# Layer 0's GELU written as Erf and one VectorE multiplication, so that ScalarE keeps one table set

## The chip, the cores and the metric

The kernel runs on one core of a Trainium2 chip. The metric is the device time of one execution in microseconds. The engines are PE (TensorE), DVE (VectorE), ACT (ScalarE), POOL (GpSimd) and SP (SyncE, which issues DMAs).

## What is computed

The input x is 8 x 128 x 128 (batch, time, channel). Four blocks follow each other, each of the form x = x + ffn(cond(x)). Cut to what matters here, layer 0 is:

```python
# cond of layer 0 (t_emb is the condition, one row per batch element)
shared = silu(xf @ w1) * (xf @ w3) @ w2
s = sigmoid(concatenate([xf, tf]) @ router_W)
# the top 2 of s + router_bias; gates are their s, divided by the sum (1/2 each where the sum is below 1e-9)
h = gelu(einsum('nc,ech->enh', xf, W1e), approximate=False)      # 8 experts, 128 wide
routed = einsum('ne,enc->nc', combine, einsum('enh,ehc->enc', h, W2e))
c = (shared + routed) / 3
# ffn of layer 0
probs = sigmoid(c @ router_w.T)
# the top 2 of probs, divided by their sum
h = square(relu(einsum('td,edw->tew', c, W1e)))
x = x + einsum('ted,te->td', einsum('tew,ewd->ted', h, W2e), combine)
```

Layer 1 is a GRU over time and a feed-forward part with 8 experts and exact GELU, layer 2 a gated linear part with 8 experts and exact GELU, and layer 3 a tanh recurrence followed by a 12-expert mixture with exact GELU.

## The kernel before

The 1024 columns (time x batch) are cut into four chunks of 256 (32 steps of time). The work up to layer 2 is a list of units, and each takes one slot n. C units are the cond part of layer 0 (C0 and C1 the silu pair, C2 to C5 two experts each), F units its feed-forward part, A and B units layers 1 and 2. Every engine goes through the slots in the same order. The first 44 slots (A_START = 44) hold layer 0: C0 to C5 of the first chunk are slots 0 to 5, then C0 to C3 of the second chunk (6 to 9), F0 to F5 of the first (10 to 15), C4 and C5 (16, 17); the third chunk's C0 to C3 are 18 to 21, F0 to F5 of the second 22 to 27, C4 and C5 28 and 29; the last chunk's C0 to C5 are 30 to 35, F of the third chunk 36 to 41, and two F units of the last 42 and 43.

In slot n PE does the up product of unit n (`project`, into PSUM bank U[n % 2], two halves in quarters 0 and 1) and the down product of unit n - 2 (`down`, into Y, in quarters 2 and 3). `project(n)` first waits until unit n - 2 has been taken out of its bank (`wait_hidden`, L1684). ACT applies the curve of unit n (`hidden`, L775) in quarter 2: for C0 a tanh into `act`, for C2 to C5 `Gelu` straight into `gated` (L783), for F units relu and, in quarter 3, the square (L797). DVE finishes C0 and C1 in `finish(n - 1)` (L1150) at quarter 0 of slot n. With the expert weights as scalars it adds the down products of slot n - 3 to accumulators `acc_a` and `acc_b` (L955, four operations of 128x128 in C2 to C5 and F0 and F1, two in F2 to F5). The down of a unit waits until the adds of the unit two before it have freed its Y bank.

At slot 2, quarter 0, DVE also does the router of the cond part: `scores_c`, and `route_c` for the first two tiles (L1471 to L1475); the other six tiles follow at slots 6 to 9. `take_sums` (L1189) writes the layer's output c0, which the F units read, four slots after C5, and the logits' copy one slot later. ACT then applies the sigmoid (`sigmoid_l0`, L799) at SIG_SLOT, that is slots 10, 22, 36 and 40, and DVE ranks them in eight quarters from the next slot's quarter 1 on (`route_f_quarter`, L1242).

From slot 20 to slot 43 the first 32 steps of the GRU run between the quarters (`beat`, L98): in four steps of every three slots, PE multiplies for the gates, ACT applies two tanh (L761, L763), DVE makes `rh`, PE multiplies, ACT applies a tanh (L767), and DVE's scan gives the new state (L1041). POOL makes the part of the state that is kept. The later steps go one per slot, with A and B units.

ACT's functions come from table sets, and a load is placed ahead of the first function that the loaded set does not hold. The kernel steers this by hand for some: `table_of` (L804) applies a function to one column so that its set is loaded there. It does so for Gelu at slots 27 and 42 (GELU_AGAIN) and for Sigmoid in quarter 2 of slot 22 (SIG_LATE), where the relu of slot 22 and its square are held back to slot 23, quarter 0, behind the sigmoid. The sigmoid of the third chunk waits until slot 36, quarter 0.

Of the kernel before, what the change touches and what calls it, by code (L numbers as in the profile page):

```python
# [1 line left out]

# [5 lines left out]
ALU = mybir.AluOpType  # L8
ACT = mybir.ActivationFunctionType
# [5 lines left out]
CHUNKS = T // CT  # L15
N = CT * B
# [4 lines left out]
F = 512  # L21
# [23 lines left out]
def layer_units(stream, k, first=0, last=LU):  # L45

    return [(stream, i, k) for i in range(first, last)]


UNITS = L0_UNITS[:-HOLD] + layer_units("A", 0) + L0_UNITS[-HOLD:]  # L50
# [5 lines left out]
AT = {u: n for n, u in enumerate(UNITS)}  # L56
A_START = AT["A", 0, 0]
C3 = AT["A", 0, CHUNKS - 1]
SIG_SLOT = [AT["C", 5, k] + 5 for k in range(CHUNKS)]
SIG_SLOT[2] = AT["C", 5, CHUNKS - 1] + 1  # L60
SIG_LATE = SIG_SLOT[1]
GELU_AGAIN = AT["F", 5, 1], A_START - 2
UP_HI_SLOTS = [8, 9] + [14 + e for e in range(E - 2)], [A_START + 4 + 2 * e for e in range(E)]
W1_SLOTS = [AT[stream, i, k] for k in (1, 2) for stream, i in zip("AAABBB", (7, 10, 13, 6, 7, 10))]

# [7 lines left out]
def unit(n):  # L73

    return UNITS[n] if 0 <= n < len(UNITS) else ("", 0, 0)
# [79 lines left out]
def m_of(*name):  # L155
    return M_PRO + X.index(name)
# [16 lines left out]

def made_by_act(n):

    return sum(stream in "FAB" or stream == "C" and i > 1 for stream, i, c in UNITS[:n + 1])


class OwnOrder:
# [11 lines left out]
def adaln_ffn_program(nc, a, out):  # L191
    with ExitStack() as ctx:
        def sb(name, shape, dtype=F32, scope=ctx):
            return scope.enter_context(nc.sbuf_tensor(name, shape, dtype))
# [4 lines left out]
        def psum(name):  # L199
            return ctx.enter_context(nc.psum_tensor(name, [P, 512], F32))  # L200

        def sem(name):
            return ctx.enter_context(nc.semaphore(name))
# [45 lines left out]
        c0 = (l2_in, z1m_c0[:, N:])  # L249
        l1_x, l2_x = parts("l1_x", [P, N]), parts("l2_x", [P, N])  # L250
        gated = sb("gated", [P, 4, 512])
# [47 lines left out]
        with ExitStack() as early:  # L299
# [4 lines left out]
            silu = sb("silu", [P, 512], scope=early)  # L304
            act = sb("act", [P, 512], scope=early)
# [91 lines left out]
        U = [psum("U0"), psum("U1")]  # L397
# [15 lines left out]
        m_full, m_free = sem("m_full"), sem("m_free")  # L413
        e_full, ga_full, gd_full = sem("e_full"), sem("ga_full"), sem("gd_full")
        l3_hid = sem("l3_hid")
        set_up = sem("set_up")
        l0_sig, silu_done = sem("l0_sig"), sem("silu_done")
# [308 lines left out]
        def _(sc):  # L726
# [3 lines left out]
            def load_small(loads):  # L730
                for dst, src in loads:
                    sc.dma_start(dst, src).then_inc(ld_small, 16)
# [42 lines left out]
            def hidden(n):  # L775
                stream, i, k = unit(n)
                if (stream, i) == ("C", 1) or not stream:
                    return
                sc.wait_ge(u_full, n + 1)
                if (stream, i) == ("C", 0):  # L780
                    nc.scalar.activation(act[:, :], U[n % 2][:, :], ACT.Tanh, scale=0.5).then_inc(e_full, 1)
                elif stream == "C":
                    nc.scalar.activation(gated[:, n % 4, :], U[n % 2][:, :], ACT.Gelu).then_inc(ga_full, 1)  # L783
                elif stream == "F":
                    nc.scalar.activation(relu[:, i % 2, :], U[n % 2][:, :], ACT.Relu).then_inc(relu_done, 1)
                else:
                    for h in range(2):
                        col = (stream == "B") * E * Q + 2 * i + h
                        last = nc.scalar.activation(gated[:, n % 4, h * N:(h + 1) * N], U[n % 2][:, h * N:(h + 1) * N],  # L789
                                                    ACT.Gelu, bias=b1T[:, col:col + 1])  # L790
                    last.then_inc(ga_full, 1)

            def square_l0(n):
                stream, i, k = unit(n)
                if stream == "F":
                    sc.wait_ge(relu_done, k * 6 + i + 1)
                    nc.scalar.activation(gated[:, n % 4, :], relu[:, i % 2, :], ACT.Square).then_inc(ga_full, 1)  # L797

            def sigmoid_l0(n):  # L799
                if n in SIG_SLOT:  # L800
                    sc.wait_ge(m_free, m_of("logits", SIG_SLOT.index(n)) + 1)
                    nc.scalar.activation(sig_a[:, 0:TILES * E], score[:, 0:TILES * E], ACT.Sigmoid).then_inc(l0_sig, 1)  # L802

            def table_of(func):  # L804

                nc.scalar.activation(table[:, :], ident[:, 0:1], func)  # L806
# [47 lines left out]
            for n in range(A_START):  # L854
                for quarter in range(4):
                    gates, cand_step = beat(n, quarter)
                    if gates is not None:
                        gru_gates_of(gates)
                    if cand_step is not None:
                        gru_cand_of(cand_step)  # L860
                    if quarter == 0 and n - 1 == SIG_LATE:
                        sigmoid_l0(n - 1)
                        hidden(n - 1)
                        square_l0(n - 1)
                    if quarter == 0 and n == SIG_SLOT[2]:
                        sigmoid_l0(n)
                    if quarter == 0 and n in GELU_AGAIN:
                        table_of(ACT.Gelu)
                    if quarter == 2 and n == SIG_LATE:
                        table_of(ACT.Sigmoid)  # L870
                    if quarter == 0:
                        mid_copies(n)
                    if quarter == 2 and n != SIG_LATE:
                        hidden(n)
                    if quarter == 3 and n == 0:
                        load_small(small_loads[9:])
                    if quarter == 3 and n == 1:
                        sigmoid_c()
                    if quarter == 3 and n not in (SIG_LATE, SIG_SLOT[2]):
                        sigmoid_l0(n)  # L880
                    if quarter == 3 and n != SIG_LATE:
                        square_l0(n)
                    if quarter == 3:
                        up_high(n)
            for n in range(A_START, SLOTS):
# [56 lines left out]
        def _(dve):  # L942
# [6 lines left out]
            def ts(out, in0, s1, op0, s2=None, op1=None):  # L949
                if op1 is None:  # L950
                    return v.tensor_scalar(out, in0, s1, None, op0)
                return v.tensor_scalar(out, in0, s1, s2, op0, op1)

            def stt(out, in0, scalar, in1, op0, op1):
                return v.scalar_tensor_tensor(out=out, in0=in0, scalar=scalar, in1=in1, op0=op0, op1=op1)  # L955
# [194 lines left out]
            def finish(n):  # L1150

                stream, i, k = unit(n)
                if (stream, i) == ("C", 0):
                    dve.wait_ge(e_full, k + 1)
                    stt(silu[:, :], act[:, :], 1.0, U[n % 2][:, :], ALU.add, ALU.mult).then_inc(silu_done, 1)
                if (stream, i) == ("C", 1):
                    dve.wait_ge(u_full, n + 1)
                    dve.wait_ge(silu_done, k + 1)
                    stt(gated[:, n % 4, :], silu[:, :], 0.5, U[n % 2][:, :], ALU.mult, ALU.mult).then_inc(gd_full, 1)

            def add_l0(n, part):

# [17 lines left out]
            def taken(*name):  # L1180
                dve.wait_ge(m_full, m_of(*name) + 1)
                return bank_of(*name)
# [6 lines left out]
            def take_sums(n):  # L1189

                if n == MID_SLOT + 1:
                    later_set_up()
                stream, i, k = unit(n - 4)
                if (stream, i, k) == ("C", 5, 0):
                    dve.wait_ge(m_free, m_of("mid", 2) + 1)
                if (stream, i, k) == ("C", 5, 1):
                    dve.wait_ge(m_free, m_of("mid", 3) + 1)
                if (stream, i) == ("C", 5):
                    ts(c0[k % 2][:, :], taken("c", k)[:, 0:N], 1.0 / 3.0, ALU.mult).then_inc(m_free, 1)
                if (stream, i) == ("F", 5):  # L1200
                    tt(x1[:, at(k * N, N)], xT[:, at(k * N, N)], taken("f", k)[:, 0:N], ALU.add).then_inc(m_free, 1)
                stream, i, k = unit(n - 5)
                if (stream, i) == ("C", 5):
                    v.tensor_copy(score[:, 0:S], taken("logits", k)[:, 0:S]).then_inc(m_free, 1)
# [367 lines left out]
        def _(pe):  # L1572
# [111 lines left out]
            def wait_hidden(n):  # L1684
                stream, i, k = unit(n)
                if (stream, i) == ("C", 0):
                    pe.wait_ge(silu_done, k + 1)
                elif (stream, i) == ("C", 1):
                    pe.wait_ge(gd_full, k + 1)
                else:  # L1690
                    pe.wait_ge(ga_full, made_by_act(n))

# [294 lines left out]
```

## Time and profile before

| | us |
|---|---|
| median of 3 runs | 599.39 |
| lowest, highest | 598.94, 599.4 |
| the profiled execution, its time | 599.04 |
| its span, first to last instruction | 597.3 |

The profile has a page (busy time and share of each engine, the chain of work that ended last) and views of the trace: the busy time by stretches, the timeline, the instructions by line, the waits. Times in the trace are counted from the start of the span. The time of a run exceeds the span by 1.7 us here. The busy shares are means over the whole span, and this change acts only on the first 44 slots, which end near 124 us.

### The profile page before, as it was taken

To read this page: it belongs to the slowest core of one execution; us is meant where nothing else is said; L and a number is where in the kernel's file an instruction comes from. 1 tells how busy PE (TensorE), PEld (TensorE's weight loads), DVE (VectorE), ACT (ScalarE), POOL (GpSimd) and SP (SyncE) were. 2 spreads that over 40 slices of the span, in tenths; PEclk is the share of its full clock that TensorE was granted. 3 is DMA by queue.
4 is the path that set the end of the run, shared out by engine and by line. 5 is a ranking of instruction groups with operands and counts; after the bars stand their busy time and mean duration, and the time that the engine had idled before them with its cause. 6 is when DMAs were issued, how large, how long until landed. Compare 5 with 4: busy or idle time off the path is not lost.

```text
span 597.3 us, 11431 instructions
## 1 busy us (share of the span) xinstructions
PE 584.0 (98%) x3978; PEld 538.1 (90%) x3978; DVE 356.5 (60%) x1199; ACT 287.1 (48%) x955; POOL 116.9 (20%) x340
## 2 busy tenths in 40 slices
PE   8899999999999999999999999999999999999996
PEld 8789889899999999999999999989999899898995
DVE  4965666865564455555654564479696763675414
ACT  3375645645665456555565556656833323302110
POOL 3334122111111111111211110000201311312410
PEclk9999999999999999999999999999999999999999
DMA  8999900002002010001010022380502003003000
GB/s 242 318 316 138 76 4 2 2 2 73 1 1 72 2 64 10 2 19 54 17 57 2 0 73 72 71 142 3 176 1 107 6 6 107 6 6 108 8 1 9
DMA packets 55297, 35.44 MB, mean 59 GB/s; under 512 B 29976, under 2 KB 48968, under 8 KB 54728
## 3 DMA queue, kind: packets, MB, share of 16 engines
q1 hardware_dynamic: 53216, 34.23, 24.2%
q10 hardware_dynamic: 2024, 0.48, 0.4%
q8 instruction: 31, 0.51, 0.4%
q14 instruction: 26, 0.21, 0.1%
HBM read 34.06 MB, written 0.64 MB: 58 GB/s over the span
## 4 chain that ended last, share of the span: by engine, by line
PE 86%; DVE 6%; issue 4%; ACT 2%; POOL 1%; DVEq 0%; POOLq 0%
PE Y L1574 35%; PE U L1574 32%; PE HH L1574 7%; PE ZR L1574 7%; PE M L1574 3%; DVE acc_a L955 2%; POOL scaled_lo L704 1%; DVE cmp_a L947 1%; DVE rh L955 0%; ACT L806 0%; ACT L802 0%; PE M L1590 0%; ACT gated L797 0%; DVE gated L955 0%; PE Y L1604 0%
## 5 line engine op out<-in xcount | busy, mean ns | idle before, releaser
L789 ACT ACTIVATE gated<-U,b1T 128x256 f32<-128x256 f32 x256 | 106.5, 472 | 0.3 <-PE U L1574 0.2
L1574 PE MATMUL U<-l_x_hi,l_up_hi 128*128 128x256 f32 x256 | 83.5, 326 | 0.0
L674 POOL TENSOR_SCALAR zh<-zr_s 128x8 f32<-128x8 f32 x128 | 26.4, 206 | 238.9 <-ACT zr_s L763 238.9
L771 ACT ACTIVATE h<-ZR,rnn_b 128x8 f32<-128x8 f32 x128 | 34.3, 268 | 78.9 <-PE ZR L1574 77.3
L1574 PE MATMUL U<-l_x_lo,l_up_hi 128*128 128x256 f32 x256 | 72.0, 281 | 0.0
L1574 PE MATMUL U<-l_x_hi,l_up_lo 128*128 128x256 f32 x256 | 71.7, 280 | 0.0
L1041 DVE TENSOR_TENSOR_SCAN h_gru<-blend,cand_keep 128x16 f32<-128x16 f32 x128 | 25.0, 195 | 77.7 <-ACT cand_keep L767 75.7
L1574 PE MATMUL Y<-gated,l_dn 128*128 128x256 f32 x256 | 69.8, 396 | 0.2 <-DVE product L947 0.2
L767 ACT ACTIVATE cand_keep<-HH 128x8 f32<-128x8 f32 x128 | 22.8, 178 | 92.4 <-PE HH L1574 92.4
L1574 PE MATMUL U<-scaled_hi,l_up_hi 128*128 128x256 f32 x192 | 57.6, 300 | 0.0
L1574 PE MATMUL U<-scaled_lo,l_up_hi 128*128 128x256 f32 x192 | 54.3, 283 | 0.0
L1574 PE MATMUL U<-scaled_hi,l_up_lo 128*128 128x256 f32 x192 | 54.2, 282 | 0.0
L1574 PEld LDWEIGHTS HH<-h_gru,gru_u 128*128 128x128 f32 x256 | 46.5, 190 | 7.7 <-DVE h_gru L1041 2.2
L1574 PEld LDWEIGHTS ZR<-h,rnn_w 128*128 128x128 f32 x256 | 43.3, 189 | 6.7 <-ACT h L771 2.3
L1574 PEld LDWEIGHTS U<-l_x_hi,l_up_lo 128*128 128x128 f32 x256 | 48.8, 191 | 0.1
L1574 PEld LDWEIGHTS U<-l_x_hi,l_up_hi 128*128 128x128 f32 x256 | 48.7, 190 | 0.1
L955 DVE SCALAR_TENSOR_TENSOR acc_a<-Y,mix,acc_a 128x128 f32<-128x128 f32 x96 | 33.7, 351 | 24.4 <-PE Y L1574 21.9
L1574 PEld LDWEIGHTS U<-l_x_lo,l_up_hi 128*128 128x128 f32 x256 | 48.2, 188 | 0.0
L1574 PEld LDWEIGHTS HH<-rh,gru_u 128*128 128x128 f32 x256 | 39.1, 188 | 9.7 <-DVE rh L955 7.9
L1574 PEld LDWEIGHTS Y<-gated,l_dn 128*128 128x128 f32 x256 | 44.1, 191 | 4.1 <-issue 0.6
L1574 PE MATMUL ZR<-h_gru,gru_u 128*128 128x8 f32 x256 | 47.1, 256 | 0.0
L1574 PE MATMUL HH<-rh,gru_u 128*128 128x8 f32 x256 | 39.8, 228 | 2.4 <-DVE rh L955 2.0
(277 smaller groups left out, 1352.4 us busy)
## 6 DMA issues: line engine op xcount, KB each, us to landing
l_bc<-dw SPq DMA_DIRECT2D x4, 1536.0 KB, 6.4
stage<-L_ffn_W_dram SPq DMA_DIRECT2D x4, 768.0 KB, 15.1
w_raw<-L_ffn_W_dram SPq DMA_DIRECT2D x12, 256.0 KB, 5.6
l_bc<-dmix SPq DMA_DIRECT2D x9, 256.0 KB, 3.8
l_bc<-dmix SPq DMA_DIRECT2D x3, 768.0 KB, 5.4
l_up_raw<-L_ffn_W_dram SPq DMA_DIRECT2D x1, 2048.0 KB, 11.5
l_up_raw<-L_ffn_w_dram SPq DMA_DIRECT2D x1, 2048.0 KB, 12.9
l_weighted<-dmix SPq DMA_DIRECT2D x3, 512.0 KB, 4.7
```

What stands on the lines that cost most here:

```text
L674: own(nc.gpsimd.tensor_scalar(zh[:, :], zr_s[:, 0, :], -0.5, 0.5, ALU.mult, ALU.add))
L704: nc.gpsimd.tensor_tensor(out=scaled[1][:, 2 * j:2 * j + 2, :].rearrange("p e n -> p (e n)"), in0=source[:, j % 2, :], in1=scaled[0][:, 2 ...
L767: nc.scalar.activation(cand, HH[:, at(N + step % CT * B, B)], ACT.Tanh).then_inc(gru_cand, 1)
L771: nc.scalar.activation(h3[:, at((step + 1) * B, B)], ZR[:, at(step % CT * B, B)], ACT.Tanh, bias=rnn_b[:, 0:1]).then_inc(rnn_h, 1)
L789: last = nc.scalar.activation(gated[:, n % 4, h * N:(h + 1) * N], U[n % 2][:, h * N:(h + 1) * N], ACT.Gelu, bias=b1T[:, col:col + 1])
L947: return v.tensor_tensor(out=out, in0=in0, in1=in1, op=op)
L955: return v.scalar_tensor_tensor(out=out, in0=in0, scalar=scalar, in1=in1, op0=op0, op1=op1)
L1041: v.tensor_tensor_scan(out=h_gru[:, at(step % CT * 2 * B, 2 * B)], data0=blend[:, :], data1=cand_keep[:, :], initial=0.0, op0=ALU.mult, op ...
L1574: return nc.tensor.matmul(out, lhsT, rhs, start=start, stop=stop, skip_group_check=shared)
```

## The change

C2 to C5 no longer use Gelu. ACT writes Erf(u / sqrt(2)) into the one buffer `act`, and DVE multiplies (act + 1) by U into `gated`, which is twice the GELU. The factor is made good in c0 (1/6 in place of 1/3), and C1's product is doubled too (1.0 in place of 0.5). The hand-made table steps go: the sigmoids of the second and third chunk stand in quarter 3 of slots 22 and 34 (SIG_SLOT as computed), the relu and square of slot 22 in their own quarters, and one Gelu is applied to a column at the end of slot 43. ACT waits, before each curve of a C unit, for DVE to have read the last one out of `act`. PE waits for C units on `gd_full` (DVE) in place of `ga_full` (ACT).

```diff
-SIG_SLOT[2] = AT["C", 5, CHUNKS - 1] + 1
-SIG_LATE = SIG_SLOT[1]
-GELU_AGAIN = AT["F", 5, 1], A_START - 2
...
 def made_by_act(n):
-    return sum(stream in "FAB" or stream == "C" and i > 1 for stream, i, c in UNITS[:n + 1])
+    return sum(stream in "FAB" for stream, i, c in UNITS[:n + 1])
+
+def made_by_dve(n):
+    return sum(stream == "C" and i > 0 for stream, i, c in UNITS[:n + 1])
+
+def curves_of_c(n):
+    return sum(stream == "C" and i != 1 for stream, i, c in UNITS[:n + 1])
...
                 sc.wait_ge(u_full, n + 1)
+                if stream == "C":
+                    before = max((m for m in range(n) if unit(m)[0] == "C" and unit(m)[1] != 1), default=None)
+                    if before is not None and unit(before)[1] == 0:
+                        sc.wait_ge(silu_done, unit(before)[2] + 1)
+                    elif before is not None:
+                        sc.wait_ge(gd_full, made_by_dve(before))
...
                 elif stream == "C":
-                    nc.scalar.activation(gated[:, n % 4, :], U[n % 2][:, :], ACT.Gelu).then_inc(ga_full, 1)
+                    nc.scalar.activation(act[:, :], U[n % 2][:, :], ACT.Erf, scale=math.sqrt(0.5)).then_inc(e_full, 1)
...
-                    if quarter == 0 and n - 1 == SIG_LATE:
-                        sigmoid_l0(n - 1)
-                        hidden(n - 1)
-                        square_l0(n - 1)
-                    if quarter == 0 and n == SIG_SLOT[2]:
-                        sigmoid_l0(n)
-                    if quarter == 0 and n in GELU_AGAIN:
-                        table_of(ACT.Gelu)
-                    if quarter == 2 and n == SIG_LATE:
-                        table_of(ACT.Sigmoid)
...
+                    if quarter == 3 and n == A_START - 1:
+                        table_of(ACT.Gelu)
...
-                    dve.wait_ge(e_full, k + 1)
+                    dve.wait_ge(e_full, curves_of_c(n))
...
-                    stt(gated[:, n % 4, :], silu[:, :], 0.5, U[n % 2][:, :], ALU.mult, ALU.mult).then_inc(gd_full, 1)
+                    stt(gated[:, n % 4, :], silu[:, :], 1.0, U[n % 2][:, :], ALU.mult, ALU.mult).then_inc(gd_full, 1)
+                if stream == "C" and i > 1:
+                    dve.wait_ge(e_full, curves_of_c(n))
+                    stt(gated[:, n % 4, :], act[:, :], 1.0, U[n % 2][:, :], ALU.add, ALU.mult).then_inc(gd_full, 1)
...
-                    ts(c0[k % 2][:, :], taken("c", k)[:, 0:N], 1.0 / 3.0, ALU.mult).then_inc(m_free, 1)
+                    ts(c0[k % 2][:, :], taken("c", k)[:, 0:N], 1.0 / 6.0, ALU.mult).then_inc(m_free, 1)
...
-                elif (stream, i) == ("C", 1):
-                    pe.wait_ge(gd_full, k + 1)
+                elif stream == "C":
+                    pe.wait_ge(gd_full, made_by_dve(n))
```

## Rows read from the trace of the kernel before

**Rows 1.** The page: busy time by engine, and the chain that ended last by engine.
```profile
PE 584.0 (98%) x3978; PEld 538.1 (90%) x3978; DVE 356.5 (60%) x1199; ACT 287.1 (48%) x955; POOL 116.9 (20%) x340
...
PE 86%; DVE 6%; issue 4%; ACT 2%; POOL 1%; DVEq 0%; POOLq 0%
```

**Rows 2.** Busy by stretch: length, each engine's busy us (instructions), clock, DMA share, GB/s.
```profile
12.10:21.00 8.90, 7.46 (x46) 6.42 (x46) 7.89 (x26) 5.07 (x8) 3.37 (x5) 1.00 1.13 325
...
38.00:51.70 13.70, 13.67 (x95) 12.88 (x95) 7.12 (x23) 9.16 (x16) 7.62 (x6) 1.00 1.32 211
```

**Rows 3.** The chain in order of time, 8 to 62 us: start, us, what.
```profile
21.01 1.13 PE Y L1574 x8
22.14 0.86 PE U L1574 x4
23.01 0.89 PE Y L1574 x8
...
29.33 1.12 PE U L1574 x4
...
31.08 1.28 ACT L802
...
32.62 0.85 DVE cmp_a L947
...
38.03 1.13 PE Y L1574 x8
...
51.75 0.18 ACT zr_s L761
```

**Rows 4.** The timeline, 12 to 52 us: start, us, engine, line, operation [idle before <- releaser].
```profile
15.17 1.13 PE L1574 MATMUL U<-h,l_up 128*128 128x256 f32 x4 [0.25 <-ACT gated L783]
...
19.40 0.17 DVE L947 TENSOR_TENSOR comb_x<-comb_x,mask 128x16 f32<-128x16 f32 x1
...
19.61 2.54 DVE L955 SCALAR_TENSOR_TENSOR acc_a<-Y,comb_x,acc_a 128x128 f32<-128x128 f32 x8
```

**Rows 5.** By line or tile: ns min/median/max, first and last start in us.
```profile
L783 ACT ACT_TABLE_LOAD  x2: 1283/1283/1283, 13.2 to 43.6; - x2
...
L802 ACT ACT_TABLE_LOAD  x2: 1283/1283/1283, 31.1 to 99.0; - x2
...
L806 ACT ACT_TABLE_LOAD  x3: 1283/1283/1283, 59.1 to 117.0; - x3
...
L781 ACT ACTIVATE act<-U x4: 592/597/597, 8.5 to 83.2; 128x512 f32<-128x512 f32 x4
L955 DVE SCALAR_TENSOR_TENSOR silu<-act,U x4: 661/684/689, 11.1 to 84.3; 128x512 f32<-128x512 f32 x4
```

**Rows 6.** Busy by stretch: slots 20, 23, 27, 33, 35, 38, 42.
```profile
51.79:54.59 2.80, 2.71 (x19) 2.17 (x18) 2.34 (x10) 1.44 (x6) 0.52 (x3) 1.00 1.69 142
...
60.55:64.11 3.56, 3.18 (x23) 2.62 (x22) 2.40 (x11) 2.97 (x11) 0.80 (x4) 1.00 1.51 121
...
73.10:76.13 3.03, 2.77 (x21) 2.48 (x20) 1.31 (x7) 2.81 (x9) 0.65 (x4) 1.00 0.05 12
...
89.92:92.60 2.68, 2.68 (x22) 2.57 (x22) 1.41 (x6) 1.20 (x5) 1.29 (x6) 1.00 0.00 0
...
95.89:98.65 2.76, 2.76 (x23) 2.56 (x22) 2.25 (x11) 1.41 (x6) 0.59 (x3) 1.00 0.00 0
...
104.51:107.97 3.46, 3.15 (x23) 2.54 (x22) 3.13 (x16) 1.98 (x8) 0.70 (x4) 1.00 0.00 0
116.62:119.64 3.02, 2.76 (x20) 2.46 (x20) 2.12 (x11) 2.80 (x9) 0.68 (x4) 1.00 0.00 0
```

**Rows 7.** The timeline of ACT at slot 44.
```profile
124.04 0.18 ACT L761 ACTIVATE zr_s<-HH 128x8 f32<-128x8 f32 x1 [1.43 <-PE HH L1574]
```

**Rows 8.** PE's waits, 0 to 52 us: total us, times, longest us.
```profile
PE Y L1574 <- DVE acc_a L955: 2.3, 3, 1.2
```

**Rows 9.** The timeline of PE at the start.
```profile
1.58 3.78 PE L1574 MATMUL HH<-ident 128*128 128x128 f32 x16 [1.58 <-POOL ident L603]
```

More of the change, by code:

```diff
@@ L1 @@
 from contextlib import ExitStack
+import math
 import concourse.bass as bass
@@ L860, in _ @@
                         gru_cand_of(cand_step)
-                    if quarter == 0 and n - 1 == SIG_LATE:
-                        sigmoid_l0(n - 1)
-                        hidden(n - 1)
-                        square_l0(n - 1)
-                    if quarter == 0 and n == SIG_SLOT[2]:
-                        sigmoid_l0(n)
-                    if quarter == 0 and n in GELU_AGAIN:
-                        table_of(ACT.Gelu)
-                    if quarter == 2 and n == SIG_LATE:
-                        table_of(ACT.Sigmoid)
                     if quarter == 0:
                         mid_copies(n)
-                    if quarter == 2 and n != SIG_LATE:
+                    if quarter == 2:
                         hidden(n)
@@ L878, in _ @@
                         sigmoid_c()
-                    if quarter == 3 and n not in (SIG_LATE, SIG_SLOT[2]):
+                    if quarter == 3:
                         sigmoid_l0(n)
-                    if quarter == 3 and n != SIG_LATE:
+                    if quarter == 3:
                         square_l0(n)
+                    if quarter == 3 and n == A_START - 1:
+                        table_of(ACT.Gelu)
                     if quarter == 3:
```

## The prediction

> **What bounds the kernel now.** I read the page first: PE is busy 98% of the span, DVE 60%, ACT 48%, and the chain that ended last is 86% PE, 6% DVE and 2% ACT [rows 1]. So ACT's table loads can give back only what lies on that 2%, or what they delay on the small share of the others. The change acts only before slot 44, that is before about 124 us. I therefore read that stage in parts. From 12.1 to 21.0 us DVE is busy 7.89 of 8.90 us and PE 7.46, so the opening of layer 0 is DVE's. From 38.0 to 51.7 us PE is busy 13.67 of 13.70 us and DVE 7.12: there DVE has room [rows 2].
>
> The chain in order of time says the same. From the first router's scores to 21.01 us it runs through DVE (routing of the first chunk, then the expert adds), and PE resumes at 21.01. It is PE's to 29.33; then relu, a table load of 1.28 us at 31.08 (the chain counts all of it), and DVE again from 32.62 until PE takes over at 38.03 [rows 3]. The third view is the engines' timeline: PE starts U of slot 4 at 15.17, having waited 0.25 us (so from 14.92, when the down product of slot 1 ends) for ScalarE's GELU of slot 2. DVE's last routing operation of the first two tiles starts at 19.40 and ends at 19.57 [rows 4]. Between these two rows lies the main step.
>
> **What goes.** In layer 0 ACT loads a table eight times after the first Tanh: once for the first sigmoid (L739), and seven more: two at L783, two at L802, three at L806, 1283 ns each [rows 5]. After the change Sigmoid, Tanh, Erf, Relu, Square and Copy share one set, so the load at L739 stays and one Gelu load at the end of slot 43 takes the place of these seven: six fewer, 7.7 us of ACT. What each is worth at the end:
> - The load at 13.2 delays U of slot 4 by 0.25 us at most, and what follows waits longer for DVE: 0.
> - The load at 31.08 is on the chain. Without it the sigmoid waits for the logits' copy, which DVE will deliver late (below). I count it there.
> - The load at 43.6 lies where PE is the bound [rows 2]: 0.
> - In the GRU stage a slot takes 2.68 us when nothing disturbs it (slot 33). Slots 27, 36 and 42, each of which has a load between two GRU gates, take 3.02 to 3.04 (the first and the last of the three stand in [rows 6]): 0.35 us each, 1.05 in all, not 1.28 each, since the GRU's own round trip hides the rest.
> - The load at 59.1 ends before the next gates are due. But slot 23 takes 3.56 us, with the sigmoid, the held-back relu and its square packed ahead of the GRU candidate. Spread as the change has them, I take back 0.5 (between 0 and 0.88, its excess over slot 33).
> - The new load at slot 43 fills ACT's idle time there: the next gates start at 124.04 after 1.43 us of idle ACT [rows 7]; 1.28 and the one-column Gelu (0.2) fill it: 0.1 us lost.
>
> Of the load itself the rows show 1283 ns, and the chain has nothing else at it: 31.08 and 1.28 us, then the sigmoid and at 32.62 the compare [rows 3]. The Trainium skill ("ScalarE: Activation LUTs", What ACT_TABLE_LOAD costs) agrees on 1283 ns but adds about 1380 ns of drain for each switch. By that figure the three loads inside the GRU would give an estimated 4.1 us more, and the forecast would be no change. Between the load's end (32.36) and the compare lie 0.26 us, which hold the sigmoid and no such drain, so the sum goes by 1283 ns; the other case is among the rivals.
>
> **What comes.** Sixteen expert units (four in each chunk) get a DVE product of 128x512 from act and U, and the same shape took 684 ns [rows 5]. ScalarE's Erf takes a GELU's place; the trace has no Erf, and I take 0.60 from the Tanh of this shape (597 ns, [rows 5]) as for the GELU: between nothing and twice this, a bound that matters for two of them. More important is where DVE finds them. finish(n - 1) stands at quarter 0 of slot n, and at slot 2 DVE does the whole routing of the first two tiles inside that quarter. So the product of slot 2 can't start before 19.57 us, though its Erf is ready near 14. PE's U of slot 4 waits for gated of slot 2 (it reuses that bank), and everything is queued behind it. The steps, with PE's 0.87 us for a project and 0.89 for a down ([rows 3], at 22.14 and 23.01):
> - Slot 2's product 19.6 to 20.3. PE starts U of slot 4 at 20.4 in place of 15.17.
> - `act` is one buffer, so the Erf of slot 3 waits for that product: 20.3 to 20.9; product 21.0 to 21.65. Erf of slot 4 21.7 to 22.3; product 22.3 to 23.0. DVE idles 0.67 us before each of these two.
> - Then slot 2's four adds (eight took 2.54 us, [rows 4]) to 24.3, slot 5's product to 25.0, slot 3's adds and a mask to 26.5. PE's down of slot 5, which waits for these adds, starts at 26.5 in place of 23.01: +3.5.
> - DVE goes on without a pause and has some 0.3 us more delay than PE by then; slot 8's product (0.7) goes in ahead of c0: PE's U of slot 10 starts at 33.9 in place of 29.33, +4.6. Slot 9's product goes ahead of the logits' copy: +5.3 there. Now the load at 31.08 is missing, so the sigmoid is at +4.0 and the first compare, 32.62 before, near 36.8: +4.2. GpSimd's subtractions will stand elsewhere beside that compare (0.85 us here), which may give up to 0.4 back.
> - From there to 38.03 DVE is dense with unchanged work, then PE is the bound until the GRU starts: the products of slots 16 and 17 fit beside it. I take +4.0 at 51.7 us, with 2.5 and 5.5 as ends (the first if PE and DVE overlap better by two products, the second if no part of the shift is recovered).
>
> In the GRU stage eight products remain. In slots 21, 22, 29, 30, 33 and 34 they meet few adds. Before, slot 20 has such a product already (C1 of the third chunk) and takes 2.80 us, against 2.76 for slot 35 without one [rows 6]. This is 0.04, but DVE's products stand at other places of the GRU beat in four of the six, where DVE must have the reset ready some 0.8 us after the update. Ends 0 and 0.68; I take 0.2 each, nearer to the row: 1.1. Slots 35 and 36 get a product, four adds and, since the third sigmoid moves from slot 36 to 34, its ranking; slot 38 loses it. Ranking with four adds cost 3.46 against 2.76 in slots 38 and 35, so 0.7 moves and the product adds some 0.2 each: +0.4. Sum of the stage: 1.1 + 0.4 + 0.1 - 1.05 - 0.5 = 0.05. The new waits of ACT on silu_done and gd_full bind only in slots 3 to 5: elsewhere the product runs a quarter or two before ACT's next curve. SP's queue isn't touched and its loads are not awaited by PE here. POOL's GRU work follows ACT's gates.
>
> **The sum.** +4.0 + 0.05 = +4.05 on the profiled execution's 599.04 (span 597.3): 603.1, and 0.35 us more on the median of 599.39: 603.4. Behind slot 44 PE is the bound (98% overall), so the shift reaches the end whole.
>
> **Rivals.**
> - The slow clock, chance 0.25. PE would be idle from 14.9 to 20.4 us, 5.5 us, which nothing in the trace before resembles: its waits for DVE up to 52 us are three of 2.3 us together, the longest 1.2 [rows 8]. At the start, out of idleness, 16 products took 3.78 us, 236 ns each, against 111 ns for the same shape at 23.01 [rows 3, 9]: the lower level of 1.2 GHz by their durations, though the granted clock reads 1.00. If PE drops to it, U of slot 4 and the next two products take about 0.9 us more each, and slot 3's adds end some 2 us later: 605.4. The Trainium skill ("TensorE: Matmul & The Clock Gate", Part 1) says that an idle PE returns to half rate and needs sustained work to leave it.
> - The loads win, chance 0.10: if each of the four loads that stand in the GRU stage gave its full 1.28 (5.1 with slot 23), the one at 31.08 too, and the first slots lost only two products (1.4) because PE's queue isn't held up: 599.4 - 6.4 + 1.4 + 1.1 = 595.5. It decides where the product of slot 2 runs before the routing; the order of the code speaks against it.
> - The loss is caught, chance 0.05: PE's three waits before 38 us, 2.3 us together [rows 8], absorb most of it and the GRU gains 1.5, or a switch holds ACT longer than its row shows, so that the three slots give their 1.28 each and more: 599.6 to 600.5 either way.
> - The change doesn't do what it says, 0.05: if Erf and Sigmoid lie in different sets, the sigmoids keep their loads: +1.3 to +2, 605.
> - Otherwise, 0.55, the forecast.
>
> **The numbers.** A measurement of this kernel can tell 0.2%, 1.2 us, from no change. The low end takes the smaller opening loss (2.5 in place of 4.0) and products in the GRU slots that cost nothing but in 35 and 36 (1.1 less), plus half of what slot 23 and the three loads may still give beyond my price: 600.3. The high end is the clock case with 1.1 of the 1.5 by which the opening may be dearer: 606.5. The winning case and the tails are left out, nearly 2 in 10. Faster 0.10, same 0.05, slower 0.85.
>
> **What would show it.** Right: a DVE product at 19.6 directly behind comb_x; PE idle some 5 us before U of slot 4; PE's U of slot 10 near 34 and the first GRU gates near 55.7 (51.75 before, [rows 3]); three table loads in all; slots 27, 36 and 42 near 2.7. Slow clock: products of the 128x128 shape near 230 ns after 20.4. Wrong: U of slot 4 before 17 us, or a gain of over 2 us between the first gates and slot 44, or more than three loads.

## The result, and the profile after

The changed kernel takes 604.56 us (median of 6) against 599.69 for the kernel before in the same runs; the ratio is 1.0094, with a 95% interval from 1.0083 to 1.0105. By the ratio it is 5.0 to 6.3 us slower. The two medians alone give 4.9 us (1.0081), a little under that interval, so the size is known to some 0.7 us. The profiled execution took 604.4 us, its span is 602.7.

The page, the two lines that answer to [rows 1], and the clock row of its second part:

```profile
PE 586.1 (97%) x3978; PEld 540.2 (90%) x3978; DVE 365.1 (61%) x1215; ACT 280.8 (47%) x947; POOL 117.8 (20%) x340
...
PEclk9799999999999999999999999999999999999999
...
PE 89%; DVE 8%; issue 2%; ACT 1%; POOL 0%; DVEq 0%; POOLq 0%
```

ACT lost 6.3 us of work and DVE gained 8.6, and the chain moved the same way: ACT 2% to 1%, DVE 6% to 8%. New is the 7 in the row of the clock. The timeline of the opening shows where it comes from (start, us, engine, line, operation, idle before and what ended it); it answers to [rows 4]:

```profile
13.51 0.60 ACT L798 ACTIVATE act<-U 128x512 f32<-128x512 f32 x1
...
19.69 0.17 DVE L954 TENSOR_TENSOR comb_x<-comb_x,mask 128x16 f32<-128x16 f32 x1
...
19.89 0.69 DVE L962 SCALAR_TENSOR_TENSOR gated<-act,U 128x512 f32<-128x512 f32 x1
20.64 2.07 PE L1584 MATMUL U<-h,l_up 128*128 128x256 f32 x4 [5.41 <-DVE gated L962]
20.68 0.60 ACT L798 ACTIVATE act<-U 128x512 f32<-128x512 f32 x1 [6.57 <-DVE gated L962]
21.31 0.69 DVE L962 SCALAR_TENSOR_TENSOR gated<-act,U 128x512 f32<-128x512 f32 x1 [0.72 <-ACT act L798]
22.50 1.91 PE L1584 MATMUL Y<-l_dn,gated 128*128 128x128 f32 x8
```

Slot 2's Erf is ready at 14.11, its product stands behind the last routing operation and starts at 19.89, and PE sat idle for 5.41 us before U of slot 4. These four matmuls then take 2.07 us (1.13 in [rows 4]), and the eight of the down 1.91, where the timeline of the kernel before has 1.05:

```profile
16.13 1.05 PE L1574 MATMUL Y<-l_dn,gated 128*128 128x128 f32 x8
```

The stretches of the same opening (length, busy us and instructions of PE, PEld, DVE, ACT and POOL, granted clock, DMA share, GB/s) give the reason:

```profile
12.40:15.20 2.80, 2.80 (x18) 2.43 (x17) 2.28 (x8) 1.34 (x3) 0.00 (x0) 1.00 1.19 286
15.20:20.60 5.40, 0.03 (x1) 0.00 (x0) 4.96 (x14) 0.00 (x0) 3.35 (x5) 0.74 1.11 334
20.60:22.50 1.90, 1.86 (x4) 1.51 (x5) 0.69 (x1) 0.60 (x1) 0.00 (x0) 0.50 1.05 376
22.50:24.50 2.00, 2.00 (x10) 2.00 (x9) 0.73 (x2) 0.60 (x1) 0.00 (x0) 0.50 1.20 288
24.50:26.00 1.50, 1.50 (x11) 1.34 (x11) 1.18 (x4) 0.53 (x1) 0.00 (x0) 0.96 1.05 270
```

While PE idles its granted clock falls, and from 20.6 to 24.5 us it is 0.50, the lower level of 1.2 GHz, although PE is busy again. Only then does it return.

PE's first matmul of each slot gives the shift against the kernel before, slot by slot. The first of slot 20 starts at 57.37 (51.79 before, +5.58), that of slot 24 is at +4.97, of slot 28 at +4.29, of slot 31 at +4.73, of slot 35 at +4.74, of slot 38 at +6.51, of slot 39 at +5.84 and that of slot 44, at 130.10, is at +5.54. So the opening costs 5.58 and the GRU stage nothing (-0.04), and behind slot 44 the rest of the span takes back only 0.1. Three stretches of it, slots 23, 27 and 42, answer to three of [rows 6], and slots 35 and 36 stand behind them:

```profile
66.12:69.08 2.96, 2.92 (x23) 2.57 (x22) 2.41 (x11) 1.94 (x7) 0.78 (x4) 1.00 1.13 98
77.89:80.42 2.53, 2.53 (x21) 2.43 (x20) 1.38 (x7) 1.55 (x7) 0.65 (x4) 1.00 0.00 1
122.45:125.19 2.74, 2.74 (x20) 2.47 (x20) 2.12 (x11) 1.54 (x7) 0.71 (x4) 1.00 0.00 0
100.63:104.41 3.78, 3.11 (x23) 2.64 (x22) 3.34 (x14) 1.45 (x6) 0.80 (x4) 1.00 0.01 2
104.41:107.91 3.50, 2.81 (x21) 2.40 (x20) 3.22 (x14) 1.37 (x6) 0.40 (x2) 1.00 0.00 0
```

Slot 23 takes 2.96 us in place of 3.56, slot 27 2.53 in place of 3.03, slot 42 2.74 in place of 3.02: there the loads and the packed sigmoid are gone. In slot 35 DVE is busy 3.34 of 3.78 us and in slot 36 3.22 of 3.50: each has a product, four adds and a part of the ranking.

### The profile page after: what moved, and what is told of

Its sections match the earlier page's. It is cut to its first block, busy times and chain, and to the rows that moved or that the text cites. A ratio compares the mean times of both kernels' runs of the same rounds, so it can differ in the third digit from the quotient of the medians.

```text
span 602.7 us, 11458 instructions
## 1 busy us (share of the span) xinstructions
PE 586.1 (97%) x3978; PEld 540.2 (90%) x3978; DVE 365.1 (61%) x1215; ACT 280.8 (47%) x947; POOL 117.8 (20%) x340
## 4 chain that ended last, share of the span: by engine, by line
PE 89%; DVE 8%; issue 2%; ACT 1%; POOL 0%; DVEq 0%; POOLq 0%
PE Y L1584 36%; PE U L1584 33%; PE ZR L1584 8%; PE HH L1584 7%; PE M L1584 3%; DVE acc_a L962 2%; DVE gated L962 1%; DVE cmp_a L954 0%; DVE rh L962 0%; PE Y L1614 0%; DVE comb_x L954 0%; DVE l_x_lo L954 0%; PE M L1600 0%; DVE h_gru L1048 0%; DVE cmp_b L954 0%
```

## The experiments

In the readings below, "shift" is the start of a slot's first matmul against the kernel before. The first layer's start itself varies by some 0.4 us between executions (U of slots 2 and 3 starts at 12.13 in the kernel before, 12.44 in the changed one, between 11.96 and 12.47 in the others); where shifts of the opening are compared, this is taken out and the number is called net. The changed kernel's net shift at slot 20 is 5.58 - 0.31 = 5.27.

A net shift is good to some 0.3 to 0.5 us, since DVE's routing starts by its own path. Its first operation on the sigmoid's output starts at 13.24 in the kernel before. It is 0.31 later in the changed kernel and 0.36 in pe_warm, which agrees with U of slot 2. But it is 0.61 later in products_early (U of slot 2: 0.31) and 0.45 later in sig36 (U of slot 2: 0.09 earlier). Each profile is also one execution, and not always a typical one.

**pe_warm: products that nothing reads, in PE's wait.** Each of the 24 calls makes two matmul instructions of the trace, x48.

```diff
+                    if (n, quarter) == (4, 0):
+                        keep_busy(24)
                     if quarter < 2:
                         project(n, (quarter,))
```

> The changed kernel, with 24 idle products (128x128 into HH, which nothing reads before the GRU) in PE's queue ahead of U of slot 4, to fill its wait from 15.2 to 20.6 us. Theory A (the drop of the granted clock to 0.50 after the wait is a cost of its own): U of slot 4 still starts near 20.6, its four matmuls take some 1.0 us in place of 2.07, the down of slot 5 starts near 26.9 in place of 28.8, and the time is 1.3 to 2.0 us under the change, about 603.0. Theory B (DVE bounds these slots anyway, the clock costs nothing): 604.4 to 604.8.

602.81 us, ratio 1.0056 (1.0041 to 1.0071). The timeline and the stretch after the wait:

```profile
15.15 5.52 PE L1584 MATMUL HH<-ident 128*128 128x128 f32 x48
20.69 1.13 PE L1584 MATMUL U<-h,l_up 128*128 128x256 f32 x4
...
20.60:22.50 1.90, 1.89 (x13) 1.71 (x13) 0.72 (x2) 0.96 (x2) 0.00 (x0) 1.00 1.05 378
```

U of slot 4 starts at the same time (20.69) and takes 1.13 us in place of 2.07, the clock stays at 1.00, and slot 20 is at +4.04, net 3.74. The wait is the same, only its effect on the clock is gone: theory A, and the clock's own share of the opening is 5.27 - 3.74 = 1.53 us in these two executions.

**product2_early and products_early: the products of slots 2 and 3 inside the routing.**

```diff
-                        finish(n - 1)
+                        if n not in (3, 4):
+                            finish(n - 1)
                         if n == 2:
                             scores_c()
                             route_c(range(TILES), (0,))
+                            finish(2)
                             add_l0(1, 0)
+                            finish(3)
                             route_c(range(TILES), (3, 4, 5))
```

This is products_early; product2_early has finish(2) alone there and leaves finish(3) at its place.

> The changed kernel, with the product of slot 2 moved on DVE's queue from behind the routing of the first two tiles (slot 3) to its middle, right behind the ranking (slot 2). Nothing else moves. Theory A (the place of this product in DVE's order opens the wait): U of slot 4 starts near 16.7, no clock drop, but the product of slot 3 still stands behind the routing, so U of slot 5 waits to about 21.3; 2.0 to 3.0 us under the change, about 602. Theory B (the loss is DVE's work alone, sixteen products of 0.69): no change, 604.6, since DVE does the same work.

601.57 us, ratio 1.0039 (1.0025 to 1.0052). Theory B (no change) is refuted. U of slot 4 starts at 16.65 and U of slot 5 at 20.68, after waits of 1.40 and 2.01 us, as expected. But the clock did fall, a little later:

```profile
18.00:20.00 2.00, 0.68 (x7) 0.48 (x5) 1.73 (x9) 0.00 (x0) 1.60 (x4) 1.00 1.02 375
20.00:22.00 2.00, 1.32 (x5) 1.14 (x6) 1.27 (x3) 0.60 (x1) 0.00 (x0) 0.85 1.04 385
22.00:24.00 2.00, 2.00 (x10) 1.92 (x9) 1.93 (x7) 0.60 (x1) 0.00 (x0) 0.50 1.19 290
```

So "no clock drop" was wrong: two shorter waits with some work between them bring it as well.

> The changed kernel, with the products of slots 2 and 3 both put into the middle of slot 2's routing on DVE (behind the ranking, and behind the copy of slot 1's down). PE then has no wait over 2.5 us and its clock stays. What is left of the opening's loss is the six products of slots 2 to 5, 8 and 9 on a DVE that is the bound. Theory A (this work is most of the +4.0 that stay without the clock drop): the first GRU slot still starts 2.7 to 3.3 us later than before (51.79), 601.0 to 601.8. Theory B (the order on DVE's queue was most of it): it starts less than 1.5 us later, under 600.5.

600.07 us, ratio 1.0010 (1.0001 to 1.0019): almost all of the loss is gone, and theory A is refuted in size. Slot 20 is at +2.05, net 1.74, where 2.7 to 3.3 was expected. Theory B's time (under 600.5) holds; its bound of 1.5 for slot 20 is missed by the start of U of slot 2 and met by the start of the routing (2.05 - 0.61 = 1.44). PE's granted clock is 1.00 from 12.4 to 32.0 us. With the same operations as the changed kernel and no clock drop, the order on DVE's queue is worth 3.74 - 1.74 = 2.00 us, or 2.2 by the start of the routing. Six products of 0.69 (4.1 us of DVE) cost 1.4 to 1.7 when they stand where they are ready, since part of them falls into idle time of DVE; that this is the reason is argued, not measured. The medians put more on the order: pe_warm lies 3.6 us over the kernel before and this run 0.7, and its profiled execution (600.62) was one of its slowest. So the order is the largest part by either measure, and its size is 2 to 3 us.

**gelu0: the first chunk as before.** ACT's GELU for slots 2 to 5, Erf and products from slot 8 on.

```diff
+                elif stream == "C" and k < 1:
+                    nc.scalar.activation(gated[:, n % 4, :], U[n % 2][:, :], ACT.Gelu).then_inc(ga_full, 1)
                 elif stream == "C":
                     nc.scalar.activation(act[:, :], U[n % 2][:, :], ACT.Erf, scale=math.sqrt(0.5)).then_inc(e_full, 1)
```

(with the factors and the counts of the semaphores to match)

> The changed kernel, with the expert units of the first chunk (slots 2 to 5) as before: GELU by ACT straight into gated, no product, factors 1/3 and 0.5 for this chunk; one table load more at slot 2 and one at slot 8. Products start at slot 8. Theory A (the opening's loss sits in slots 2 to 5, and slots 8 and 9 cost their two products, 1.4, less the 0.4 that the missing load at slot 10 gives): the first GRU slot starts 0.8 to 1.2 us later than before, and with the GRU stage as in the change 600.2 to 600.8. Theory B (the loss is spread evenly over the products): two thirds of it go, still with the clock at 1.00: about 601 to 602.

598.70 us, ratio 0.9989 (0.9980 to 0.9998). Slot 20 is at +0.27, net 0.08: better than theory A. The whole opening's loss sits in slots 2 to 5; the products of slots 8 and 9 together with the missing load at slot 10 cost nothing measurable. PE's starts show both: the shift grows by 0.60 from U of slot 9 to U of slot 10 (1.4 was priced) and shrinks by 0.60 from slot 12 to 13 (0.4 was priced).

**no_products: the loads alone.** Erf goes straight to gated, and the factor (1 + erf) times u is left out.

```diff
-                    nc.scalar.activation(act[:, :], U[n % 2][:, :], ACT.Erf, scale=math.sqrt(0.5)).then_inc(e_full, 1)
+                    nc.scalar.activation(gated[:, n % 4, :], U[n % 2][:, :], ACT.Erf, scale=math.sqrt(0.5)).then_inc(ga_full, 1)
...
-                if stream == "C" and i > 1:
-                    dve.wait_ge(e_full, curves_of_c(n))
-                    stt(gated[:, n % 4, :], act[:, :], 1.0, U[n % 2][:, :], ALU.add, ALU.mult).then_inc(gd_full, 1)
```

> The table loads alone: the changed kernel, with Erf written by ACT straight into gated as GELU was, and no product by DVE; waits as before. It leaves out the factor (1 + erf) times u of the expert units of layer 0, so the outputs differ. Six loads fewer, nothing added. Theory A (priced by what the GRU's slots gave back in the change: 0.6 + 0.2 + 0.5 + 0.35 + 0.3, and 0.7 to 1.0 for the load at 31.08): 2.5 to 3.3 us under the kernel before, about 596.7. Theory B (each load gives its 1.28): 7.7 under, 592. Theory C (ACT's idle time hides them): 599.4.

596.72 us, ratio 0.9955 (0.9938 to 0.9971), 2.5 us under the kernel before: theory A. Six loads of 1283 ns, with the sigmoid, relu and square of slot 23 spread out again, are worth 2.5 of their 7.7 us, so not even their full 1283 ns shows up at the end. Nor does ACT stand still behind a load: in the kernel before the one at 31.08 ends at 32.36, and the sigmoid starts at 32.38. The Trainium skill ("ScalarE: Activation LUTs", What ACT_TABLE_LOAD costs) has a longer switch, and no row here shows one. By slots: net -0.19 at slot 20, then -0.61 in slot 23, -0.50 in slot 27, +0.14 over slots 35 to 38 with the ranking moved, -0.27 in slot 42; -1.63 at slot 44. The remaining 0.5 of the span lies behind it. Against the one trace of the kernel before, the traces of all changed kernels gain there: 0.12 us near 134 us and 0.33 near 319 in all eleven, and 0.35 between 203 and 208 in all but this one. The code is the same there; whether this comes with that one execution or with the change isn't shown. It concerns sizes of up to 0.8 us read from spans, not the shifts up to slot 44.

**sig36: the third sigmoid back at slot 36.**

```diff
+SIG_SLOT[2] = AT["C", 5, CHUNKS - 1] + 1
...
+                    if quarter == 0 and n == SIG_SLOT[2]:
+                        sigmoid_l0(n)
...
-                    if quarter == 3:
+                    if quarter == 3 and n != SIG_SLOT[2]:
                         sigmoid_l0(n)
```

> The changed kernel, with the third chunk's sigmoid back at slot 36, quarter 0 (no table load there now), so that its ranking lies in slots 37 and 38 and no longer in 35 and 36 beside two products and two split copies. Theory A (the moved ranking costs): the slots 35 to 38, which lose 1.8 us against before in the change (shift 4.71 to 6.51) and get 0.7 back in slot 38, lose under 0.4: 0.7 to 1.1 us under the change, about 603.7. Theory B (the two products with four adds cost it, wherever the ranking is): within 0.3 of the change.

603.41 us, ratio 1.0064 (1.0045 to 1.0083). Over slots 35 to 38 the shift goes from +5.55 to +5.63, where the changed kernel goes from +4.74 to +5.84: 0.08 against 1.10. Theory A; but no_products, with the same moved ranking and no products, lost only 0.14 there, so the moved ranking costs this much only beside the products. The median is 1.15 us under the changed kernel's. The profiled execution is the longest of the four and gains only 0.36, since in it the low clock lasted longer:

```profile
20.80:24.00 3.20, 3.20 (x11) 2.84 (x12) 1.18 (x2) 1.19 (x2) 0.00 (x0) 0.50 1.13 324
24.00:27.00 3.00, 3.00 (x13) 2.64 (x13) 1.41 (x5) 0.60 (x1) 0.00 (x0) 0.56 1.07 289
```

Its slot 20 is at +6.39. The four executions spread from 602.15 to 604.04.

**erf_late, erf_late_no_pre, erf_late_slot20: Erf for the last two chunks alone.** As gelu0 with k < 2 for the first branch and the sigmoid at slot 36; erf_late has besides

```diff
+                    if quarter == 3 and n in (9, 17):
+                        table_of(ACT.Sigmoid)
```

and the two others only slot 17 and only slot 9 there.

> Erf and products for the third and fourth chunk alone, where DVE has room; the first two chunks keep GELU. The Sigmoid's set is loaded ahead of need at the ends of slots 9 and 17, and the third sigmoid stays at slot 36. Theory A (terms measured so far): opening -0.3 to -0.5 (load at 31.08 off the chain), GRU stage -1.05 as with the sigmoid at 36: 1.3 to 1.6 us under the kernel before, ratio 0.9973 to 0.9978. Theory B (the eight GRU products need the idle that the later opening gave): 0.5 us or less under it.

599.34 us, ratio 0.9996 (0.9987 to 1.0005): theory A's gain is not there. The time alone would fit theory B (0.5 or less), but not its reason, since the loss lies ahead of the GRU slots. Slot 20 is at +0.27 although U of slot 10 was early (28.89 against 29.33). The chain in order of time shows what came in between (start, us, what):

```profile
42.64 1.28 ACT L799
...
45.56 1.28 ACT L824
46.85 0.20 ACT table L824
47.05 0.52 ACT l_up_hi L852
47.57 0.49 ACT act L797
...
49.41 0.43 DVE x L961
49.84 0.14 issue
49.98 0.79 PE ZR L1591 x3
```

ACT's tanh of slot 18 waits behind two loads, DVE's silu waits for it, x1 stands behind the silu, and PE waits 1.03 us for x1 at the GRU's inputs. In the kernel before the load at 43.6 left this chain at most 0.36 us of room (x1 ends at 49.56, and by its chain PE's first GRU input starts at 49.92; by its timeline it starts at 49.71 already). A second load uses it up and more.

> The same without the early load at the end of slot 9, so that the load stands ahead of the sigmoid of slot 10, as before. It prices that one load: 0.3 to 0.5 us over the run with it, that is 0.9 to 1.1 under the kernel before. If the load is hidden in fact, both are equal.

599.86 us, ratio 1.0005 (0.9996 to 1.0014): the load ahead of slot 10's sigmoid is worth about 0.5 us by the medians. The intervals overlap. The traces agree on it: with the early load the shift goes from -0.44 at slot 12 to -0.98 at slot 13, without it it stays at 0.32, so the load is worth 0.54. The 0.9 to 1.1 under the kernel before that was expected fails as it did in erf_late. Slot 20 starts at 52.06 in the one profiled execution and at 53.36 in the other; 0.75 of these 1.3 us is there at U of slot 4 already, ahead of any difference between the two.

> Erf for the third and fourth chunk alone, as before, but without the early load at the end of slot 17: the set is loaded at the first Erf, slot 20, inside the GRU beat. Theory A (that early load held ACT's tanh of slot 18, so DVE's silu and, behind it, x1 of the first chunk, for which PE's GRU inputs waited 1.03 us): no such wait, the first GRU slot starts 0.3 to 0.8 us earlier than in the kernel before, slots 20 to 22 lose 0.3 to 0.7 to the load, slot 44 starts 1.0 to 1.5 earlier, ratio 0.9970 to 0.9980. Theory B (the wait comes from DVE's own work): the wait stays and the run with the early load is not beaten.

599.08 us, ratio 0.9995 (0.9985 to 1.0005). The wait is gone and slot 20 starts at 51.54 (-0.25), so theory A on its cause holds; its time (0.9970 to 0.9980) doesn't. The load inside the beat cost 0.74 us in slot 20 alone, where 0.3 to 0.7 was allowed for slots 20 to 22, and the profiled execution (600.51) shows the clock again:

```profile
54.00:56.00 2.00, 1.33 (x7) 1.05 (x6) 1.07 (x5) 0.83 (x4) 0.40 (x2) 0.86 1.56 130
56.00:58.00 2.00, 2.00 (x10) 1.82 (x10) 0.64 (x3) 0.70 (x3) 0.19 (x1) 0.50 1.37 157
```

PE was busy 1.33 of 2 us there, and the shift grows from -0.25 at slot 20 to +2.14 at slot 22. The longest wait in these 2 us is 0.67. The eleven executions spread from 598.34 to 601.35, three of them at 600.5 or more.

**gelu0_sig36: the parts that pay.** The first chunk's GELU on ACT, everything else Erf, the third sigmoid at slot 36 (the edits of gelu0 and sig36).

> GELU by ACT for the first chunk (as in the run before), Erf and products from slot 8 on, and the third sigmoid at slot 36. Theory A (the terms add: opening near 0, 0.08 after the common start is taken out, and GRU stage -1.05): slot 44 starts 0.8 to 1.1 us earlier than before, ratio 0.9970 to 0.9983, about 597.9. Theory B (as in the run with Erf for the late chunks alone, something else takes the gain of the ranking back): as the run with the sigmoid at 34, 0.9989.

597.76 us against 599.55, ratio 0.9967 (0.9955 to 0.9980): faster than both kernels. Slot 44 is at -0.78, a little short of the expected 0.8 to 1.1, and the rest of the 1.8 us by the medians lies behind it, where the source isn't shown (see no_products); over slots 35 to 38 the shift goes from -0.59 to -0.50, where gelu0 went from -0.57 to +0.51. PE's waits in it (total, times, longest):

```profile
PE Y L1589 <- DVE acc_a L967: 1.8, 2, 1.2
...
PE U L1589 <- DVE l_in L963: 0.7, 1, 0.7
```

No wait in the opening is longer than in [rows 8], and none is for a product.

## Why the prediction was right or wrong

The direction and the range held. The time did not come from the case that I thought likeliest but from the rival with the slow clock, which I had at 0.25 and 605.4; by the ratio the change costs 5.6 us on 599.39, 605.0. In the changed kernel with PE's wait filled (pe_warm, 602.81) the likeliest case's 603.4 nearly comes true.

- **The opening, priced +4.0.** Without the clock drop it is +4.04 at slot 20 (pe_warm), of which 0.30 is the later start of that execution. The steps came out as written: product at 19.89 (19.6 forecast), U of slot 4 at 20.64 (20.4), PE idle for 5.41 us (5.5). U of slot 10, forecast near 34, starts at 35.50, and in pe_warm at 33.97. The cause was named rightly, the product's place behind the routing, and is shown: moving two products gives at least 2.00 us back. The size of DVE's plain work was not: I would have put it at 2.7 to 3.3, and it is 1.4 to 1.7.
- **The clock.** This is the step that failed in the likeliest case: I took 5.5 us of idle PE to leave the clock alone with twice the chance of the other way. The profiled execution shows 0.50 behind it, and filling the wait gives 1.53 us back; I had priced the drop at 2.0. Where the low clock lasted to near 27 us (sig36's profiled execution) slot 20 is 0.8 later than in the changed kernel, so 2.0 lies within what one wait can cost here. The Trainium skill ("TensorE: Matmul & The Clock Gate", Part 1) says the same of an idle PE, and I should have given it more weight than a trace in which no such wait occurs.
- **Loads.** Slots 27 and 42 gave 0.50 and 0.28 (0.35 each priced), slot 23 gave 0.60 (0.5). The new load at slot 43 cost nothing (0.1). Loads alone are worth 2.5 us. Leaving the longer switch out of the sum was right. Slot 36 can't be read alone; its 0.35 belongs to the moved ranking below.
- **Products in the GRU slots.** Slots 21, 22, 33 and 34 cost 0.03 together or less, slots 29 and 30 cost 0.18 and 0.25: 0.43 in place of 1.1. The row of slot 20 was the better guide than my reckoning of DVE's free time between update and reset.
- **The moved ranking.** Slots 35 to 37 lost 1.02 + 0.46 + 0.29 and slot 38 gave back 0.67: +1.10. The forecast for the same four slots was +0.4 and, for the load gone from slot 36, -0.35: 0.05. I added the product to the ranking's price from slot 38; together they make DVE the bound in slots 35 and 36, where it is busy 3.34 of 3.78 and 3.22 of 3.50 us. That it takes both is shown by two runs: with the ranking back in its place and the products there, the stretch costs 0.08 (sig36), and with the ranking moved and no products 0.14 (no_products). The two last errors, -0.67 and +1.05, cancel by luck, with 0.19 that slot 25 gave: -0.04 measured, 0.05 forecast.
- **The low end of the range.** Its sum doesn't close: 603.4 - 1.5 - 1.1 is 600.8, and half of what slot 23 (0.38) and the three loads (0.93 each) might still give is 1.6, so by its own terms it is 599.2, not 600.3. Nothing that was measured turns on it.

## What to carry to other kernels

Before work is moved to another engine, look up where it will stand in that engine's queue, not only how much idle time the engine has: two products of 0.69 us behind the routing cost some 2 us by their place and 1.5 us by the clock; with both among the routing the whole opening costs 1.4 to 1.7. A table load is worth what the step behind it waits, here a third of its length on the mean of six, and a hand-placed load can use up the last few tenths of a microsecond of another chain's room. A part-by-part change lets the paying parts be kept: one chunk's GELU and one sigmoid left where they were turn +0.9% into -0.3%.

## What the runs showed of the hardware beyond this

The granted clock fell to 0.50 after one wait of 5.41 us, after waits of 1.40 and 2.01 us with work between them (product2_early), and in one execution of erf_late_slot20 where PE was busy 1.33 of 2 us and waited 0.67 at the longest. It stayed at 1.00 in products_early, whose two waits for products are 2.5 us together. With the same opening in two kernels, it stayed low until about 24.5 us in one execution and near 27 in another, so the cost of the same wait varies from run to run. And at the very start of the kernel before, 16 products took 236 ns each ([rows 9]) while the record of the granted clock reads 1.00: the record shows the later drops told here, and not this first stretch.
